# Splitting every 125-partition transfer as 120 + 5 partitions in place of 112 + 13

## The chip, the core and the metric

The kernel runs on one core of a Trainium2 chip. The metric is the time of one execution on the device, in microseconds (us). Each time is the median of several runs.

## What is computed

The reference is a small network of eight residual blocks over 3125 nodes with 256 features each and 50,000 directed edges (sorted by target). Layer normalisation precedes each block:

```
x = x + attention_4_heads(norm(x))          # L0 gnn, over the edges and self loops
x = x + mixture_of_8_experts(norm(x))       # L0 ffn, hidden 256, two best experts
x = x + two_attention_layers(norm(x))       # L1 gnn, 4 heads, then 1 head of 256
x = x + recurrence(norm(x))                 # L1 ffn
x = x + three_convolutions(norm(x))         # L2 gnn, adjacency product, bias, relu
x = x + mixture_of_8_experts(norm(x))       # L2 ffn, hidden 1024
x = x + one_convolution(norm(x))            # L3 gnn
x = x + mixture_of_8_experts(norm(x))       # L3 ffn, hidden 512
```

## The kernel before

3125 nodes are 25 tiles of 125 rows. Almost every array in SBUF therefore has 125 partitions (`P = 125`, `T = 25`), one node of a tile in each. All plain transfers are begun by SyncE, on one queue, in the order of its program; row gathers and scatters by index are begun by GpSimd on another.

- The first two attention layers (`by_edges`) go over 25 blocks of edges. GpSimd gathers 17 lists of 128 feature rows for a block (line 842). Beside it a class `Adjacency` builds the dense adjacency tile of each block and stores it in two arrays in DRAM: `NEG` (a mask, line 637) and `ADJ16` (counts as float16, line 639), 3125 numbers of two bytes in each partition.
- The third attention layer (`dense_attention`) loads both back (lines 1352, 1387 and 1486).
- The convolutions load `ADJ16` tile by tile into a ring of nine buffers (line 2444). In the three-layer one GpSimd adds the self loops to each tile as it lands (line 2454), so its instructions show when a tile is there.
- The features are stored for the gathers (line 769), x is loaded at the start in five parts (line 1969).
- A mixture first stores its normalised rows to `rows_x` in five parts (line 3779), then loads the rest of its second weights if it is the one with hidden size 1024 (line 3298), and runs 56 slots of 128 rows through the experts. GpSimd scatters each slot's result to `rows_y`. When the last scatter has landed (wait at line 3613), SyncE begins ten loads, two for each of five parts of five tiles (line 3619; line 3091 in the first mixture, where the following layer's front is joined to it). VectorE adds each part into x with ten operations (line 3729), and in the last mixture SyncE stores a part of the output when it has been added (line 3624).

All of these transfers go through one helper, `two_starts`. It begins the transfer in two pieces over partitions, each with its own completion count of 16, and everyone who waits for it waits for 32.

Of the kernel before, what the change touches and what calls it, by code (L numbers as in the profile page):

```python
# [5 lines left out]
P, T = 125, 25  # L6
# [117 lines left out]

def two_starts(e, out, src, sig):

    for lo, hi in ((0, 112), (112, P)):
        e.dma_start(out[lo:hi], src[lo:hi]).then_inc(*sig.by(16))  # L128


# [363 lines left out]
class Adjacency:  # L494
# [139 lines left out]
    def sync(self, e, t):  # L634
        m = self.order(t)
        e.wait_ge(*self.neg_made.at(m + 1))
        two_starts(e, self.k.NEG[t], self.mask[:, :], self.neg_out)
        e.wait_ge(*self.cols_out.at(7 * (m + 1)))
        two_starts(e, self.k.ADJ16[t], self.cols[:, :, :].rearrange("p t i -> p (t i)"), self.adj_out)
# [117 lines left out]
class ToTable:  # L757
# [5 lines left out]
    def sync(self, e):  # L763
        h = self.heads
        rows = self.k.HR.rearrange("(t p) c -> p t c", p=P)
        for i0, i1 in ((0, 4), (4, 7), (7, 10), (10, 12), (12, 13)):
            t0, t1 = 2 * i0, min(2 * i1, T)
            e.wait_ge(*h.out.at(i1))
            two_starts(e, rows[:, t0:t1, :], h.HA[:, t0:t1, 0:h.terms + h.H], self.out)
# [3178 lines left out]
```

## Time and profile before

| | |
|---|---|
| Median of 3 runs | 4234.94 us (4234.51 to 4237.27) |
| Time of the profiled execution | 4236.11 us |
| Its span in the profile | 4234.3 us |
| TensorE matmuls busy | 3471.0 us, 82% of the span |
| VectorE busy | 2679.7 us, 63% |
| GpSimd busy | 1295.1 us, 31% |
| Plain queue (q1) | 116800 packets, 251.73 MB, 21.5% of what 16 DMA engines could do |

The profile's page gives busy time by engine, the chain that ended last, and the costliest groups of instructions. PE is TensorE, DVE VectorE, ACT ScalarE, POOL GpSimd, SPq the sequencer of SyncE. A time in a row is counted from the start of the span. "DMA share" is the mean busy share of the core's 16 DMA engines in a stretch; it is made from packet durations, so it can come out a little over 1.

### The profile page before, as it was taken

The page shows a single profiled execution, that of the slowest core. Times are in us where ns is not written, and L with a number is a line of the kernel's source. Part 1 is how long each engine was busy: PE and PEld are TensorE (multiplying, and loading weights), DVE is VectorE, ACT ScalarE, POOL GpSimd, SP SyncE. Part 2 cuts the span into 40 slices and gives each one's busy share as a digit, 9 for nine tenths or more (in the row PEclk, how much of TensorE's full clock was granted, in tenths as well). Part 3 has the DMA queues.
Part 4 walks back from the last instruction along what each step waited for, and adds up shares of the span by engine and source line. Part 5 has one row for each costly group of instructions (what it writes and reads, how often), then busy time and mean ns, then how long its engine had stood idle before and what let it go on. Part 6 is the DMA issues. An engine that isn't in the chain of part 4 may idle for free. (4 is left out here: it accounts for less than half of the span.)

```text
span 4234.3 us, 63960 instructions
## 1 busy us (share of the span) xinstructions
PE 3471.0 (82%) x22424; PEld 2902.0 (69%) x22424; DVE 2679.7 (63%) x6841; ACT 1627.8 (38%) x4215; POOL 1295.1 (31%) x1348
## 2 busy tenths in 40 slices
PE   4777775775777788998899999799997899959695
PEld 3556664653555566784888888655597799959695
DVE  6799997556888878973888888732136333353544
ACT  2354442232444435561666666621102233310231
POOL 6777771637777720000000000000000222200263
PEclk8778877986888889999999999899998999979898
DMA  5455553344555555600000000245555211163424
GB/s 158 136 146 161 146 151 102 97 136 127 144 159 145 151 151 152 147 1 15 1 1 1 2 1 1 47 108 125 141 141 182 76 37 38 32 153 97 150 72 131
DMA packets 178026, 419.53 MB, mean 99 GB/s; under 512 B 58688, under 2 KB 103410, under 8 KB 177216
## 3 DMA queue, kind: packets, MB, share of 16 engines
q1 hardware_dynamic: 116800, 251.73, 21.5%
q0 software_dynamic: 60928, 164.04, 13.7%
q8 instruction: 162, 2.65, 0.3%
q14 instruction: 136, 1.11, 0.1%
HBM read 331.25 MB, written 84.36 MB: 98 GB/s over the span
## 5 line engine op out<-in xcount | busy, mean ns | idle before, releaser
L842 POOL DMA_INDIRECT sb<-features,sb x850 | 840.1, 988 | 262.3 <-issue 258.1
L2137 PE MATMUL ps<-sb 128*128 128x125 f32 x5184 | 635.6, 279 | 71.2 <-DVE sb L2201 70.1
L2137 PEld LDWEIGHTS ps<-sb 128*128 128x128 f32 x5184 | 595.0, 192 | 111.8 <-DVE sb L2201 110.5
L3742 ACT ACTIVATE sb<-ps,sb 128x128 f32<-128x128 f32 x784 | 220.9, 376 | 545.0 <-PE ps L3662 545.0
L2168 ACT ACTIVATE sb<-ps 128x125 f32<-128x125 f32 x1296 | 330.6, 273 | 223.2 <-PE ps L2137 194.7
L1211 PE MATMUL ps<-sb 128*125 128x260 f32 x1700 | 388.0, 387 | 13.1 <-PEq L1209 12.7
L3662 PE MATMUL ps<-sb 128*128 128x128 f32 x3136 | 383.1, 277 | 3.1 <-DVE sb L3705 1.8
L1211 PEld LDWEIGHTS ps<-sb 128*125 128x125 f32 x1700 | 320.0, 190 | 94.0 <-issue 41.4
L3662 PEld LDWEIGHTS ps<-sb 128*128 128x128 f32 x3136 | 369.0, 194 | 3.9 <-DVE sb L3705 2.1
L3676 PE MATMUL ps<-sb 128*128 x1568 | 368.0, 381 | 2.6 <-ACT sb L3742 2.6
L3676 PEld LDWEIGHTS ps<-sb 128*128 128x128 f32 x1568 | 286.7, 191 | 35.4 <-issue 3.1
L3639 POOL DMA_INDIRECT rows_y<-sb x168 | 191.6, 1141 | 382.0 <-DVE sb L3717 368.3
L1527 PE MATMUL ps<-sb 125*125 125x257 f32 x1250 | 282.0, 388 | 20.2 <-DVE sb L1594 12.4
L619 PE MATMUL ps<-sb 128*125 128x392 bf16 x850 | 242.4, 466 | 66.5 <-PEq L617 65.1
L1527 PEld LDWEIGHTS ps<-sb 125*125 125x125 f32 x1250 | 238.5, 192 | 62.0 <-DVE sb L1594 15.5
L2545 PE MATMUL ps<-sb 125*128 125x500 f16 (+1 forms) x1400 | 275.7, 352 | 0.0
L2565 PE MATMUL ps<-sb 125*125 125x256 f16 x2500 | 273.4, 273 | 0.0
L2565 PEld LDWEIGHTS ps<-sb 125*125 125x125 f16 x2500 | 273.1, 136 | 0.3
L619 PEld LDWEIGHTS ps<-sb 128*125 128x125 bf16 x850 | 163.7, 201 | 133.7 <-issue 74.6
L3698 DVE COPY sb<-sb 128x512 f32 (+2 forms) x168 | 133.3, 793 | 179.3 <-PE ps L3662 178.7
L1017 DVE TENSOR_TENSOR sb<-sb,ps 128x1560 f32<-128x1560 f32 x150 | 244.3, 1684 | 1.7
L3717 DVE TENSOR_TENSOR sb<-ps,sb 128x256 f32<-128x256 f32 x168 | 71.4, 425 | 268.8 <-PE ps L3676 268.8
(380 smaller groups left out, 5296.3 us busy)
## 6 DMA issues: line engine op xcount, KB each, us to landing
sb<-adj SPq DMA_DIRECT2D x125, 683.6 KB
neg<-sb SPq DMA_DIRECT2D x25, 683.6 KB
adj<-sb SPq DMA_DIRECT2D x25, 683.6 KB
sb<-neg SPq DMA_DIRECT2D x25, 683.6 KB
sb<-in_L_ffn_W SPq DMA_DIRECT2D x16, 1024.0 KB
sb<-features,sb POOLq DMA_INDIRECT x850
sb<-rows_y SPq DMA_DIRECT2D x20, 560.0 KB
sb<-adj SPq DMA_DIRECT2D x125, 79.3 KB
```

Source lines behind the costliest of these rows:

```text
L619: r = e.matmul(k.PS[0:P, 2 + x, 0:392], dt[:, w, :], self.hots[w % 4][:, 392 * x:392 * x + 392], start=w == 0, stop=w == W - 1)
L842: e.indirect_dma_start(hgs[i % 4][:, w, :], None, k.HR, indirect(ids[i % 3][:, w:w + 1])).then_inc(*hg_in[i % 4].by(16))
L1017: e.tensor_tensor(v, v, shares[:, w0:w1, :].unsqueeze(3).broadcast_to([128, w1 - w0, 4, 65]), ALU.mult).then_inc(scaled_token.sem, 1)
L1211: m = e.matmul(k.PS[0:P, sum_bank(u), 0:260], wides[u % 2][:, w, :], hgs[u % 4][:, w, 0:260], start=w == 0, stop=w == W - 1)
L1527: m = e.matmul(k.PS[0:P, n, 0:257], work[u % 7][:, n * P:n * P + P], HA[:, j, 0:257], start=j == 0, stop=j == T - 1)
L2137: return e.matmul(sums(n, g)[:, 0, :], V[:, y, (4, 0, 5, 1, 2, 3)[g], :], self.old_h(n)[:, y, :], start=False, stop=y == 1, skip_group_che ...
L2168: e.activation(Gt[:, row, :], sums(n, g)[:, 0, :], ACT.Tanh if row >= 4 else ACT.Sigmoid).then_inc(acted, 1)
L2545: m = e.matmul(out, part[:, j, 128 * h:128 * h + 128], self.ads[:, first:first + len(ts), j * P:j * P + P], start=j == 0 and x == 0, stop= ...
L2565: m = e.matmul(self.k.PS[0:P, v % 2, 0:D], self.ads[:, self.slot(v), j * P:j * P + P], part[:, j, :], start=j == 0 and x == 0, stop=j == T ...
L3662: m = e.matmul(hidden(n, c), w1s[n % deep][:, x, c, :], xts[n % 2][:, x, :], start=x == 0, stop=x == 1)
L3676: m = e.matmul(k.PS[:, 5 + n % 2, 0:D], hts[n % 2][:, c, :], w2f[:, bass.ds(v * (nh * D) + c * D, D)], start=c == 0, stop=c == nh - 1)
L3742: m = e.activation(hts[n % 2][:, c, :], hidden(n, c), ACT.Gelu, bias=cons[n % 4][:, c:c + 1])
```

## The change

The helper cuts after 120 partitions in place of 112. The first piece grows from 112 to 120 partitions and the second shrinks from 13 to 5. The number of transfers, their bytes, their order, and every wait stay as they are.

```
 def two_starts(e, out, src, sig):
 
-    for lo, hi in ((0, 112), (112, P)):
+    for lo, hi in ((0, 120), (120, P)):
         e.dma_start(out[lo:hi], src[lo:hi]).then_inc(*sig.by(16))
```

## Rows read from the trace of the kernel before

**Rows 1.** The page, DMA queues: packets, MB, share of 16 engines.

```profile
q1 hardware_dynamic: 116800, 251.73, 21.5%
```

**Rows 2.** The DMA view of 3742.6 to 3772 us: packets, MB, share.

```profile
DMA packets 1507, 6.55 MB, mean 223 GB/s; under 512 B 248, under 2 KB 504, under 8 KB 1504
...
q1 hardware_dynamic: 1504, 6.51, 91.0%
```

**Rows 3.** The DMA view of 4192 to 4232 us.

```profile
q1 hardware_dynamic: 4810, 9.60, 86.6%
```

**Rows 4.** Windows: stretch, busy us of the engines (instructions), PEclk, DMA share, GB/s.

```profile
3243.00:3260.00 17.00, 9.19 (x82) 8.64 (x80) 13.97 (x47) 10.03 (x21) 0.00 (x0) 0.85 1.03 411
...
3714.00:3734.00 20.00, 0.00 (x0) 0.00 (x0) 13.60 (x34) 0.00 (x0) 0.00 (x0) 0.50 1.02 245
...
3955.00:3962.00 7.00, 0.00 (x0) 0.00 (x0) 6.73 (x11) 0.00 (x0) 0.00 (x0) 0.50 0.89 367
...
4196.00:4220.00 24.00, 0.00 (x0) 0.00 (x0) 16.09 (x40) 0.00 (x0) 0.00 (x0) 0.50 1.03 265
4220.00:4228.00 8.00, 0.00 (x0) 0.00 (x0) 4.14 (x11) 0.00 (x0) 0.00 (x0) 0.50 0.94 320
```

**Rows 5.** Windows of one us at the end of a burst of loads.

```profile
3733.00:3734.00 1.00, 0.00 (x0) 0.00 (x0) 1.00 (x4) 0.00 (x0) 0.00 (x0) 0.50 0.87 220
3734.00:3735.00 1.00, 0.00 (x0) 0.00 (x0) 1.00 (x4) 0.00 (x0) 0.00 (x0) 0.50 0.89 251
3735.00:3736.00 1.00, 0.00 (x0) 0.00 (x0) 1.00 (x4) 0.00 (x0) 0.00 (x0) 0.50 0.47 128
```

**Rows 6.** Waits of the whole span on DMA: total us, times, longest.

```profile
POOL sb L2454 <- DMA sb<-adj: 437.6, 75, 43.0
...
DVE sb L3729 <- DMA sb<-rows_y: 23.6, 9, 10.0
...
DVE sb L1433 <- DMA sb<-neg: 2.1, 2, 1.1
```

**Rows 7.** Windows of the edge layers and the convolutions.

```profile
1600.00:1700.00 100.00, 83.01 (x359) 69.39 (x360) 85.88 (x91) 57.61 (x69) 0.00 (x0) 0.90 0.63 157
...
3000.00:3200.00 200.00, 200.00 (x1486) 157.23 (x1484) 53.51 (x139) 19.93 (x46) 14.23 (x35) 1.00 0.51 134
...
83.00:600.00 517.00, 389.52 (x2188) 300.33 (x2188) 441.00 (x1032) 224.16 (x347) 393.98 (x403) 0.78 0.53 148
```

**Rows 8.** Timeline of POOL: start, us; when two of the first tiles are there.

```profile
2746.03 0.40 POOL L2454 TENSOR_TENSOR sb<-sb 125x125 f16<-125x125 f16 x1 [3.19 <-DMA sb<-adj]
...
2759.42 0.40 POOL L2454 TENSOR_TENSOR sb<-sb 125x125 f16<-125x125 f16 x1 [2.95 <-DMA sb<-adj]
```

**Rows 9.** The gathers of the edge layers (line 842): who waits.

```profile
L842 POOL DMA_INDIRECT sb<-features,sb x850 | 840.1, 988 | 262.3 <-issue 258.1
```

**Rows 10.** Timelines of SPq and DVE, the first mixture's parts.

```profile
898.75 8.56 SPq L128 DMA_DIRECT2D sb<-rows_y  x20
...
907.88 3.26 DVE L3103 SCALAR_TENSOR_TENSOR sb<-sb 125x256 f32<-125x256 f32 x8 [12.09 <-PEq L105]
...
913.03 2.46 DVE L3103 SCALAR_TENSOR_TENSOR sb<-sb 125x256 f32<-125x256 f32 x6
...
928.58 2.46 DVE L3103 SCALAR_TENSOR_TENSOR sb<-sb 125x256 f32<-125x256 f32 x6
```

**Rows 11.** Timeline of SPq and POOL, the mixture of hidden size 1024.

```profile
3266.89 20.48 SPq L3298 DMA_DIRECT2D sb<-in_L_ffn_W  x8
...
3288.53 1.40 POOL L3634 DMA_INDIRECT sb<-rows_x,sb  x1 [53.24 <-POOLq L105]
```

**Rows 12.** Timeline of DVE, the parts of that mixture's result.

```profile
3716.62 4.05 DVE L3729 SCALAR_TENSOR_TENSOR sb<-sb 125x256 f32<-125x256 f32 x10 [5.08 <-DMA sb<-rows_y]
...
3737.33 4.05 DVE L3729 SCALAR_TENSOR_TENSOR sb<-sb 125x256 f32<-125x256 f32 x10 [0.74 <-DMA sb<-rows_y]
```

**Rows 13.** The chain that ended last, its end.

```profile
4200.39 19.75 DMA sb<-rows_y
```

## The prediction

> **What bounds the kernel now.** I read the page first. The plain queue moves 251.73 MB in 116800 packets and fills 21.5% of the DMA engines' time [rows 1]. Transfers are thus no bound on average, and the question is where one ends a wait.
>
> The windows by stage answer most of it. In the edge layers GpSimd begins gathers without pause: of its 262.3 us idle before line 842, 258.1 are its own issue time [rows 9], at a DMA share of 0.53 [rows 7]. In the convolutions TensorE is busy all of 200 us at a share of 0.51, and in the dense attention layer the share is 0.63 [rows 7]. A transfer may get a third slower there and still be hidden.
>
> The waits of the whole span come next [rows 6]. GpSimd waits 437.6 us for adjacency tiles, but it only adds self loops there and TensorE, which uses the result, never stops. VectorE waits 23.6 us for `rows_y`, which is the end of the two later mixtures, and the chain that ended last has the same transfer in it for 19.75 us [rows 13]. These bursts are the exposed ones.
>
> **What the cut decides.** How many DMA engines share a transfer, and how many rows the busiest one has, can be counted. In the stretch of eight adjacency tiles and one weight load the queue has 1504 packets, 248 of them under 512 B [rows 2]. Eight tiles have 1000 rows and the weight load 256. The 248 small ones left are 8 x 29 + 16. At the end of the kernel ten loads of 125 rows and five stores of 625 pieces make 4375, and 4810 - 4375 = 435 = 15 x 29 [rows 3]. So each 125-row transfer ends in 29 small packets and a 128-row one in 16. I read this as 16 engines for the piece of 112 (7 rows each), 13 for the piece of 13 (one each): the busiest has 8 rows, three have 7. The end of a burst agrees: the share falls to 0.87 and 0.89 before it collapses to 0.47, about 13 of 16 [rows 5].
>
> After the change the same pattern, an equal number of rows on each of at most 16 engines, gives 15 engines with 8 rows and 5 engines with one more. The busiest have 9, five of the 16; ten have 8; one has none. If 120 rows were instead dealt unevenly over 16 engines, the busiest would still have 9.
>
> The Trainium skill, "DMA: Bandwidth & Descriptors", section "Why a DMA increments its semaphore by 16 and not by 1", has the rule: the largest number of engines up to 16 that divides the slowest dimension, and always the lowest-numbered ones. The counted 29 and 16 agree with it. By it alone, 9 rows in place of 8 make every exposed transfer 12.5% longer, which is the upper bound below.
>
> **What a row costs.** The loads of 5120-byte rows run at 245 GB/s [rows 4], 15.3 GB/s for each of 16 engines, or 334 ns a row. Weight loads of 128 rows run at 411 GB/s, which would be 199 ns for such a row. Stores of 125 rows run between 320 and 367 GB/s, 223 to 256 ns. So loads with the 112 + 13 cut are slowed by something that 128-row loads don't meet. Also, when three engines have run dry the total stays at 220 to 251 GB/s [rows 5]: part of the limit is shared, and fewer engines each run faster.
>
> **The sum**, each term with the work around it:
>
> - *Two bursts of ten loads* (after the mixtures of hidden size 1024 and 512). VectorE waits before each part, from 5.08 us for the first to 0.74 for the last [rows 12], so a later landing goes straight through. If the engine is the limit, the busiest has 10 rows more at 334 ns, +3.3 us. If the total is, the old burst is 70 rows at 334 ns plus 10 at 13 engines' share of 235 GB/s (283 ns), 26.2 us; the new one is 80 rows at 15 engines' share of 245 (313 ns), then 10 rows on five free engines at 199 ns, 27.1 us: +0.9. The rows speak for both; I take 2.0 each, +4.0.
> - *Five output stores at the very end.* The DMA engines work from the loads into the stores without a gap (shares 1.03 and 0.94) [rows 4], so one more row of 5120 bytes in each counts: 5 x 0.22 to 0.26 us, +1.2, bounds 0.5 and 1.3.
> - *Five stores of normalised rows before the mixture of hidden size 1024.* They stand in the queue before the last eight weight loads, whose issue takes 20.48 us and ends just before GpSimd may begin the experts at 3288.53 [rows 11]. Five more rows, +1.1, bounds 0 and 1.3. In the last mixture the same stores run at 367 GB/s between 3955 and 3962 beside 6.73 us of VectorE work on the placing of the rows, which the block's end waits for [rows 4]: nothing; without that cover 1.1.
> - *The first mixture's ten loads.* SyncE begins them from 898.75 on, and like the other bursts they take some 26 us; VectorE starts on the parts at 907.88, 913.03 and so on to 928.58 with no DMA wait [rows 10]. By the share of tiles before them (10 of 25, 22 of 25) these land at about 910 and 922, 3 and 6 us early. +12.5% is covered. Without that cover it is 3.3.
> - *Adjacency tiles at the front of the convolutions.* They land 13.39 us apart for four, 3.35 each [rows 8]; at 9/8 that is 3.77. With the convolutions' share at 0.51 a tile is needed only half as often: nothing.
> - *Mask and adjacency stores in the edge layers*, loads of x, masks in the dense layer: beside GpSimd's gathers or under VectorE's work; the two mask waits are 2.1 us together [rows 6]. With the ends of stages, +0.5, bounds 0 and 1.5.
>
> Together 4.0 + 1.2 + 1.1 + 0.5 = +6.8 us. The profiled execution took 4236.1 us, 1.8 more than its span, and would take 4242.9. The median of the runs shown is 1.2 lower, so 4234.9 + 6.8 = 4241.7; I say 4242 us. The terms' bounds give +2.3 to +10.7, so 4237 to 4246 for this case.
>
> **The rivals.**
>
> *A, engines meet (slower).* Loads reach only 245 of 411 GB/s, which looks like several engines writing to one entrance of SBUF at a time. With equal shares of eight rows that meeting could be regular, every row with one partner, 2 x 199 = 398 ns. A transfer then takes 8 x 398 plus a contended ninth of about 500, 3.7 us against 2.7. Twenty exposed loads cost 20 us, the first mixture's cover of 3 us is used up (+2), and stores and ends 2.8: +25, 4260. For it: the unexplained slowness is there already. Against it: in unequal queues (9 rows beside 8) partners drift apart. The Trainium skill, "SBUF — State Buffer", section "Door 1: The DMA port swizzle", gives each port two groups of four partitions, 32 apart. By that map contiguous eights make engines four apart share both their ports, which speaks for A; no trace here shows which rows an engine has.
>
> *B, the slowness goes away (faster).* 128-row loads give each engine eight rows, and 120 over 15 does too. If the eights, and not the sevens, are what runs at 199 ns, a load takes 9 x 199 ns = 1.8 us. In the burst after hidden size 1024 VectorE's waits shrink by 1.8 us for the first part and the later 4.5 of waiting vanish; at the end of the kernel similarly 1.8 + 4.0, and 1.5 from the earlier drain of the stores; the other terms stay: -13.6 + 1.6, about -12, so 4223. It decides from a row time of 8/9 x 334 = 297 ns downward. Against it: five engines still meet at the last five partitions, and the eights of a 128-row tile may be dealt differently.
>
> *C, nothing to see.* The shared limit rules throughout, extra rows fall in gaps: 0 to +2, 4236. Rows 5 speak for it, the gapless end of the kernel against it.
>
> **How the numbers follow.** About 0.2% (8.5 us) is what a measurement can tell from no change. Forecast 0.48, of which 0.16 beyond +8.5; A 0.22; B 0.18, of which 0.02 within 8.5; C 0.12. Faster 0.16, within 0.2% 0.02 + 0.12 + 0.32 = 0.46, slower 0.16 + 0.22 = 0.38. The range takes in most of B and the nearer half of A, 4224 to 4256.
>
> **What the changed profile would show.** The plain queue has 265 such transfers; 20 small packets in place of 29 in each leave 116800 - 2385 = 114415 packets. Ends of bursts fall to a share near 0.3 (five engines), with middles near 0.94. Adjacency tiles land 3.5 to 3.8 us apart; over 4.2 it is A, under 3.0 it is B. VectorE's last wait in each burst grows by about 2 us. The prediction is wrong if row time changes with the cut, if the queue of one late engine holds up SyncE's issue somewhere before a weight load, or if a landing in the edge layers turns out to hold a block.

## The result and the profile after

The changed kernel takes 4244.98 us (median of 9 runs, 4240.08 to 4247.2), the kernel before on the same chip 4234.51 us: a ratio of 1.0024 with an interval of 1.0014 to 1.0034, some 10 us slower. Its profiled execution took 4245.34 us with a span of 4243.7, 9.4 more than before.

The page's DMA queues show how the rows are dealt (compare [rows 1]):

```profile
q1 hardware_dynamic: 114415, 251.72, 22.5%
```

That is 2385 packets fewer, nine in each of the 265 transfers, as forecast. The waits of the whole span on DMA (compare [rows 6]):

```profile
DVE sb L3729 <- DMA sb<-rows_y: 30.5, 10, 11.2
...
DVE sb L1433 <- DMA sb<-neg: 4.8, 4, 2.7
...
DVE sb L154 <- DMA sb<-in_x: 2.7, 1, 2.7
...
DVE sb L3103 <- DMA sb<-rows_y: 0.8, 1, 0.8
```

The wait for `rows_y` is longer by 6.9 us. The two last lines have no partner before: the loads of x and of the first mixture were less well covered than I had thought. The burst after hidden size 1024, in the timelines of SPq and DVE (before, SPq began at 3708.95 us; compare [rows 12]):

```profile
3709.48 7.50 SPq L128 DMA_DIRECT2D sb<-rows_y  x20
```
```profile
3717.89 4.05 DVE L3729 SCALAR_TENSOR_TENSOR sb<-sb 125x256 f32<-125x256 f32 x10 [5.84 <-DMA sb<-rows_y]
...
3740.48 4.05 DVE L3729 SCALAR_TENSOR_TENSOR sb<-sb 125x256 f32<-125x256 f32 x10 [1.08 <-DMA sb<-rows_y]
```

The kernel enters the burst 0.5 us late and starts the last part 3.15 late (3737.33 before): 2.6 us lost in it. I had forecast that the last wait grows by about 2 us; it grew by 0.34 only, and the delay is spread over the five waits (5.84, 1.83, 1.53, 1.96 and 1.08 us in place of 5.08, 1.18, 1.53, 1.07 and 0.74). The windows after the burst show another microsecond. First the kernel before, then the one after, both counted from the first matmuls of the next block (columns as in [rows 4]):

```profile
3753.00:3756.00 3.00, 3.00 (x15) 2.54 (x13) 0.89 (x3) 0.71 (x2) 0.00 (x0) 0.96 0.99 233
```
```profile
3756.00:3759.00 3.00, 3.00 (x10) 2.38 (x10) 0.29 (x3) 0.53 (x2) 0.00 (x0) 0.66 0.97 219
```

TensorE, idle for 42 us ahead of this block in place of 40, is granted 0.96 of full speed in one and 0.66 in the other, both windows beginning 7.7 us after the block's first matmul. The same 16 matmuls of line 2498 take 4.99 us in place of 4.14. The longer idle time does not explain it. In two of the runs below, first the one with only the bursts changed and then the one with all but the bursts changed, the longer idle time goes with the shorter matmuls:

```profile
3748.76 2.08 PE L2464 MATMUL ps<-sb 128*128 128x256 f32 x4 [43.05 <-ACT sb L2623]
...
3755.67 4.26 PE L2498 MATMUL ps<-sb 128*125 128x256 f32 x16
```
```profile
3742.16 2.08 PE L2464 MATMUL ps<-sb 128*128 128x256 f32 x4 [38.32 <-ACT sb L2623]
...
3749.07 5.21 PE L2498 MATMUL ps<-sb 128*125 128x256 f32 x16
```

Over all 14 traces of this case the idle time is 38.3 to 43.1 us and these matmuls take 4.14 to 5.53 us, without a visible relation. So 0.9 us of this pair of traces is the clock's variation from one execution to the next, as far as can be told, and not a price of the change.

The last burst: SPq begins at 4196.84 (before 4192.59, so 4.25 late), and the last part starts at 4228.57. Before, the last two parts ran as one group of twenty operations from 4216.05 to 4224.21, so the last ten began at 4220.16:

```profile
4216.05 8.16 DVE L3729 SCALAR_TENSOR_TENSOR sb<-sb 125x256 f32<-125x256 f32 x20 [1.00 <-DMA sb<-rows_y]
```

The burst lost 4.2 us. From the end of the last sum to the end of the span it is 10.1 us before and 11.1 after. The whole account: 0.5 ahead of the first burst, 2.6 in it, 1.1 in the block behind it, 4.2 in the last burst, 1.0 in the output's stores make 9.4. It is the account of one pair of traces: where the code up to the first burst is the same as before, four traces enter it between 3708.95 and 3710.99 us, so the 0.5 us can't be told from nothing.

```profile
4228.57 4.05 DVE L3729 SCALAR_TENSOR_TENSOR sb<-sb 125x256 f32<-125x256 f32 x10 [0.39 <-DMA sb<-rows_y]
```

Windows of the middle and of the end of the first of these bursts after the change (compare [rows 4, 5]):

```profile
3715.00:3735.00 20.00, 0.00 (x0) 0.00 (x0) 12.14 (x30) 0.00 (x0) 0.00 (x0) 0.50 0.96 235
...
3738.00:3739.00 1.00, 0.00 (x0) 0.00 (x0) 1.00 (x4) 0.00 (x0) 0.00 (x0) 0.50 0.27 97
```

The middle stands near 15 of 16 engines, the end near five of 16 (0.27, at 97 GB/s), as forecast. The middle's rate fell as well. In windows of 18 us that hold no stores it is 236 from 246 GB/s in the one burst and 230 from 255 in the other.

### The profile page after: what moved, and what is told of

Read it like the earlier page. It is cut to its first block and busy times, and to the rows that moved or that the text cites. A ratio compares the mean times of both kernels' runs of the same rounds, so it can differ in the third digit from the quotient of the medians.

```text
span 4243.7 us, 63960 instructions
## 1 busy us (share of the span) xinstructions
PE 3482.4 (82%) x22424; PEld 2910.5 (69%) x22424; DVE 2683.2 (63%) x6841; ACT 1626.8 (38%) x4215; POOL 1293.9 (30%) x1348
## 5 line engine op out<-in xcount | busy, mean ns | idle before, releaser
L1211 PE MATMUL ps<-sb 128*125 128x260 f32 x1700 | 388.4, 388 | 10.2 <-PEq L1209 9.7
```

What stands on the lines that cost most here:

```text
L1211: m = e.matmul(k.PS[0:P, sum_bank(u), 0:260], wides[u % 2][:, w, :], hgs[u % 4][:, w, 0:260], start=w == 0, stop=w == W - 1)
```

## The experiments

All have the helper with another cut, unless a line is named. "Before" below is the kernel before on the same chip. A burst's length is counted from SPq's first start to the start of VectorE's last ten operations. "Tiles" are the second to the eighth adjacency tile at the front of the convolutions, 3.45 us apart before. The runs were made on several chips, where the median of the kernel before was 4234.5 to 4239.2 us; ratios compare one chip with itself, and from the traces mainly lengths are compared.

**One line alone, and all but that line.** The helper gets the cut as a parameter:

```
-def two_starts(e, out, src, sig):
-    for lo, hi in ((0, 112), (112, P)):
+def two_starts(e, out, src, sig, cut=112):
+    for lo, hi in ((0, cut), (cut, P)):
...
-    two_starts(e, got[:, n, c, :, :], best[...], got_in[n])        # line 3619
+    two_starts(e, got[:, n, c, :, :], best[...], got_in[n], 120)
```

This is the second run. The first has 120 everywhere and 112 in line 3619.

> The changed kernel, but the ten loads after each of the two later mixtures are cut 112 + 13 again; all other transfers stay 120 + 5. Theory (the cost is the later landing of these two bursts, 3.6 and 4.2 us by the two traces): about 7.8 of the 10.5 us go, so +2 to +3 us against the kernel before, ratio 1.0006; in its profile the last of the final mixture's waits ends within 1 us of the kernel before. Rival (many small later landings in the edge layers, the first mixture and the convolutions add up): most of the loss stays, +6 us or more, ratio 1.0014 or more.

> The kernel before, but only the ten loads after each of the two later mixtures are cut 120 + 5; 20 of 265 transfers. Theory (these two bursts carry the loss): +7 to +8 us, ratio 1.0018. Rival (small landings everywhere): +2 to +4 us, ratio below 1.001. If the two experiments' losses do not add to the whole loss of 10 us, the transfers change each other's timing and neither theory is complete.

Measured: 1.0005 (0.9996 to 1.0014) with the bursts left as they were, 1.0016 (1.0007 to 1.0026) with only the bursts changed. Both fit the theory and not the rival, and the two losses add to 0.21%, which agrees with the whole 0.24% within the intervals. By the centres, twenty of 265 transfers carry about two thirds of the loss.

**The same number of rows on the busiest engine, cut otherwise; one row more, cut otherwise.** `(0, 80), (80, P)` gives 15 engines 8 rows (5 + 3); `(0, 105), (105, P)` gives ten engines 9 (7 + 2).

> Every transfer cut 80 + 45: 16 engines with 5 rows, then 15 engines with 3 rows, so again 8 rows on the busiest engine as with 112 + 13, now on fifteen engines. 31 small packets in each transfer, 117330 packets on the plain queue. Theory (the number of rows on the busiest engine decides): like the kernel before, within 3 us. Rival (the time of a row depends on how many neighbouring partitions an engine has, because engines meet at one entrance of SBUF): the pace of the adjacency tiles moves from 3.4 us by more than 0.3 us either way, and the time by 5 us or more.

> Every transfer cut 105 + 20: 15 engines with 7 rows, then 10 engines with 2 rows, so 9 rows on the busiest engine as with 120 + 5, but on ten engines, 7 on five, none on one. Theory A (the busiest engine's rows at an unchanged row time): like the change, +10 us, tile pace 3.8 us. Theory B (the total rate is shared, so that late engines run faster when few are left): the ten late engines get less speed than the five of the change at the end of a burst, so +11 to +15 us. Rival (the eights of the 120 piece are slow by themselves, the sevens are not): clearly less than the change, +3 to +6 us.

Measured: 80 + 45 took 1.0021 (1.0011 to 1.003) with tiles 3.82 us apart, 105 + 20 only 1.0005 (0.9996 to 1.0014) with tiles 3.43 apart. The theory that only the rows of the busiest engine count falls: eight rows cost as much here as nine do in the change, and nine rows cost next to nothing.

**Where the blocks lie.** `(0, 5), (5, P)`, and `(0, 13), (13, P)` as its control.

> All transfers as (0, 5) and then (5, 125). The counts of rows on each engine are those of the change (five engines with 9, ten with 8), but the fifteen blocks of eight rows begin at partition 5, 13, 21 and so on in place of 0, 8, 16. Theory M (where the blocks of rows lie sets how the engines meet, and so what a row costs): with the blocks off the multiples of eight the row gets cheaper, the adjacency tiles at the front of the convolutions land under 3.6 us apart in place of 3.84, the two bursts lose less than 2.5 us each in place of 3.6 and 4.2, ratio 1.0003 to 1.0015. Rival S (the size of the blocks alone sets it, wherever they begin): tiles 3.8 apart, bursts +3.6 and +4.2, ratio 1.0020 to 1.0028, as the change.

> All transfers as (0, 13) and then (13, 125): the counts of rows are those of the kernel before (13 engines with 8, three with 7), with the sevens beginning at 13 in place of 0. It is the control of the run with the five rows first. Theory M: a small change of the row's time is possible, but sevens drift over the positions anyway, so tiles land 3.3 to 3.6 us apart (3.45 before) and the ratio is 0.9994 to 1.0006. Rival O (what counts is whether the small piece stands first in each engine's queue): a shift of the bursts by over 1 us each, of the same sign as in the run with the five rows first.

Measured: 1.0033 (1.0021 to 1.0045) with five first, tiles 4.04 us apart; 1.0004 (0.9995 to 1.0013) with thirteen first, tiles 3.33 apart. Moving the eights off the multiples of eight helped nothing; theory M falls. The bursts last as with the change (31.8 and 32.1 us). What is lost beyond it comes earlier: the kernel enters the first of them 4.1 us late, with mask waits of 7.9 us in the dense attention layer (2.1 before).

**Stores alone** (lines 637, 639, 769, 3624 and 3779 with 120).

> The kernel before with the five lines that store (masks, adjacency, features, normalised rows, output) cut at 120 and all loads at 112. Theory: the loss of the change is in its loads, and of the stores only the five at the very end count, about 1.0 us: ratio 1.0000 to 1.0005, the bursts' waits as before. Rival: the stores in the edge layers and before the mixture of hidden size 1024 cost as well (my prediction gave the latter 1.1 us): ratio 1.0006 or more, with the first gatherless stage after the edge layers shifted by over 1 us.

Measured: 1.0005 (0.9996 to 1.0014). Its bursts last 27.5 us both, as before (28.4 and 27.6), and the end behind the last sum 11.1 us in place of 10.1. That microsecond is all that its trace ties to the stores; the interval doesn't exclude a little more.

**More rows, fewer engines.** `(0, 117), (117, P)`.

> All transfers as 117 and 8 rows: 13 engines with 9 rows, of which eight get a tenth, and three engines with none. Theory M with the count: blocks of nine rows are off the multiples of eight and cost as the sevens or less (260 to 320 ns of 5120 bytes), ten rows of them make 2.6 to 3.2 us for a load in a burst, adjacency tiles 3.4 to 3.9 us apart, ratio 1.0000 to 1.0020. Rival E (thirteen engines carry less, each at the rate seen with 112 + 13): a load takes 10 x 334 = 3.3 us, bursts +6 us each, tiles over 4.2 apart, ratio 1.0030 or more. The five last stores have two rows more than before either way, about +2 us.

Measured: 1.0008 (0.9999 to 1.0017). Ten rows on the busiest engines, and the bursts last 28.2 and 28.3 us. Windows of 18 us in them show why:

```profile
3716.00:3734.00 18.00, 0.00 (x0) 0.00 (x0) 12.14 (x30) 0.00 (x0) 0.00 (x0) 0.50 0.83 251
4200.00:4218.00 18.00, 0.00 (x0) 0.00 (x0) 12.14 (x30) 0.00 (x0) 0.00 (x0) 0.50 0.83 254
```

Thirteen engines carry as much as sixteen did, 19.4 GB/s each in place of some 15.8. Rival E's bursts of +6 us don't come, so for these loads it is not each engine by itself that sets the rate; a limit shared by all would fit. For the adjacency tiles (rows of 6250 bytes) it is otherwise: they land 3.79 us apart, nearly as slow as with the change (3.84). That lies in theory M's range, as does the ratio, though the theory itself falls with the run before.

**The order of 80 and 45, and eleven rows.** `(0, 45), (45, P)` and `(0, 104), (104, P)`.

> All transfers as (0, 45) and then (45, 125): the same two sizes as in the run with 80 + 45, in the other order, so again 8 rows on fifteen engines. That run lost 0.21%, its tiles in the convolutions landed 3.82 us apart and its bursts took 22 us. Theory P (two engines that are at rows behind one entrance of SBUF share its rate, and where the blocks lie decides how often they meet; worked out with the row of 199 ns for an engine alone at its entrance, the mean load of 5120-byte rows comes to 2.68 us for 80 + 45, 2.44 for 45 + 80, 2.44 for 112 + 13 and 2.98 for 120 + 5): with the 45 rows first the loss is gone, tiles land 3.3 to 3.55 us apart, the last burst is as before, ratio 0.9992 to 1.0006. Rival Z (the size of the blocks alone, fives being slow): tiles 3.75 or more apart, ratio 1.0015 to 1.0027, as with 80 + 45.

> All transfers as 104 and 21 rows: 13 engines with blocks of 8 rows, seven of which get 3 more, so the busiest seven have 11 rows and three engines none. Theory P gives a mean load of 5120-byte rows of 3.2 us (2.44 for the cut of before): tiles about 4.2 us apart or more, each burst 5 us or more longer, ratio 1.0025 or more. Rival T (the total rate of all engines limits and the rows of the busiest hardly count, since 117 + 8 with ten rows on eight engines cost only 0.08%): tiles under 3.8 us apart, bursts under +2.5, ratio under 1.0015.

Measured: 45 first 1.002 (1.0011 to 1.0029), tiles 3.42 us apart, bursts 29.3 and 29.7 us. Theory P had the tiles right and the ratio wrong; the two orders cost the same. 104 + 21 took 1.0096 (1.008 to 1.0111). Rival T falls. Theory P had named no upper end, but its 1.0025 is far from this, and of the bursts (30.4 and 36.6 us) only the second is 5 us longer or more. The trace is that of the slowest of the four runs (4294.54 us, median 4280.89). In it the tiles land 4.6 us apart, and the mask loads of the dense attention layer have lost their cover (2.1 us before):

```profile
DVE sb L1433 <- DMA sb<-neg: 32.0, 7, 10.0
```

**The two halves of the cost**, both in line 3619 alone: three pieces `(0, 112, 120, 125)` with the wait in line 3724 raised to 96 (blocks of seven, a ninth row on five engines), and 120 rows without the rest (blocks of eight and no ninth row).

> The kernel before with only the twenty loads of the two bursts (line 3619) begun as three pieces, 112, 8 and 5 rows, and the wait for a part raised from 64 to 96. Sixteen engines keep their blocks of seven; the first five have 9 rows, three have 8, eight have 7. Theory N (the ninth row on five engines is the cost, 10 rows of 0.31 us a burst): each burst +3 us as in the run with 120 + 5 at this line, last wait chain 24 to 26 us, ratio 1.0012 to 1.0022. Rival K (the blocks of eight in step are the cost, and a ninth row among blocks of seven is not): bursts within 1 us of before, the last burst's transfer part of the chain 19 to 21 us, ratio 0.9996 to 1.0006.

> The kernel before with only the loads of line 3619 cut to their first 120 rows, in one piece; the five last rows of every tile are left out of these loads and of VectorE's sum (x keeps its value there). Fifteen engines have 8 rows each and nobody a ninth. Theory N: 10 rows less than with 120 + 5 on the busiest engines and 5 rows in 125 less in all, so each burst ends as before or up to 1 us earlier, ratio 0.9992 to 1.0003. Rival K: blocks of eight still cost, each burst 1.5 to 3 us later than before though four per cent less is loaded, ratio 1.0006 to 1.0014.

Measured: 1.0007 (0.9998 to 1.0016) with three pieces, between the theories, with bursts at most 2.0 and 2.2 us above the 27.8 that 112 + 13 takes in the mean. Part of that may be the third start, which lengthens SyncE's issue of a burst from 8.3 to 10.5 us. 120 rows only: 1.001 (1.0001 to 1.0019), in rival K's range, with bursts 2.9 and 1.0 us above the mean where K had 1.5 to 3; theory N, which had them no later than before, does not fit. Windows show where each is late. Three pieces:

```profile
3716.00:3734.00 18.00, 0.00 (x0) 0.00 (x0) 11.30 (x29) 0.00 (x0) 0.00 (x0) 0.50 1.03 245
4199.50:4217.50 18.00, 0.00 (x0) 0.00 (x0) 11.08 (x28) 0.00 (x0) 0.00 (x0) 0.50 1.03 249
```

120 rows only:

```profile
3716.00:3734.00 18.00, 0.00 (x0) 0.00 (x0) 11.71 (x30) 0.00 (x0) 0.00 (x0) 0.50 0.96 214
4203.20:4221.20 18.00, 0.00 (x0) 0.00 (x0) 12.14 (x30) 0.00 (x0) 0.00 (x0) 0.50 0.98 236
```

With the sevens the middle nearly keeps its rate and the burst is late through its end; with the eights alone the middle is slow, more so in one burst (214 GB/s) than in the other (236).

**All bursts and ends side by side.** The two columns of lengths are those after hidden size 1024 and 512; the rate is that of 18 us in the middle of each; the end is from the last sum to the end of the span.

| loads of line 3619 | busiest engine, rows | bursts, us | GB/s | stores of the output | end, us |
|---|---|---|---|---|---|
| 112 + 13 (before) | 8 | 28.4, at most 27.6 | 246, 255 | 8 rows | 10.1 |
| 112 + 13 (stores alone changed) | 8 | 27.5, 27.5 | 260, 254 | 9 | 11.1 |
| 112 + 13 (all but the bursts changed) | 8 | 27.2, 28.6 | 259, 243 | 9 | 11.1 |
| 13 + 112 | 8 | at most 27.5, at most 28.2 | 254, 252 | 8 | 10.0 |
| 120 + 5 (the change) | 9 | 31.0, 31.7 | 236, 230 | 9 | 11.1 |
| 120 + 5 (only the bursts) | 9 | 32.0, 32.5 | 226, 223 | 8 | 10.0 |
| 5 + 120 | 9 | 31.8, 32.1 | 230, 227 | 9 | 11.1 |
| 120 only | 8 | 30.7, 28.8 | 214, 236 | 8 | 10.3 |
| 112 + 8 + 5 | 9 | at most 29.8, at most 30.0 | 245, 249 | 8 | 9.9 |
| 105 + 20 | 9 | at most 27.6, 29.1 | 254, 244 | 9 | 11.2 |
| 117 + 8 | 10 | 28.2, 28.3 | 251, 254 | 10 | 12.2 |
| 80 + 45 | 8 | 30.4, 30.0 | 229, 234 | 8 | 9.9 |
| 45 + 80 | 8 | 29.3, 29.7 | 234, 234 | 8 | 10.2 |
| 104 + 21 | 11 | 30.4, 36.6 | 247, 202 | 11 | 13.3 |

("At most": VectorE ran on without a wait there.) The tiles land 3.24 to 3.45 us apart in the six traces whose loads are cut 112 + 13 or 13 + 112, 3.42 with 45 + 80, 3.43 with 105 + 20, 3.79 with 117 + 8, 3.79 and 3.84 with 120 + 5, 3.82 with 80 + 45, 4.04 with 5 + 120 and 4.62 with 104 + 21. No cut beats 112 + 13 by more than can be measured: all ratios are above 1, and those of 13 + 112, 105 + 20 and 117 + 8 have 1 in their intervals.

## Why the prediction was right, and where its sizes were off

The sign was right, and so were the packets and the places of the loss, the two bursts and the last stores. 4244.98 lies in the range of 4224 to 4256. The forecast of 4242 was 3 us short, and the ratio's centre lies just beyond the 0.2% that I had set as measurable.

- *How rows are dealt*: right. The packet count came out to the unit, and for the other cuts too: 80 + 45 has two small packets more in a transfer, 116800 + 265 x 2 = 117330 as on its page; 117 + 8 has eight fewer, 114680. The Trainium skill's rule ("DMA: Bandwidth & Descriptors", section "Why a DMA increments its semaphore by 16 and not by 1") gives each of these counts, and the traces agree.
- *Two bursts, +2.0 each*: the step that was mis-sized. "The rows speak for both; I take 2.0 each" averaged between an engine's limit (+3.3) and a shared one (+0.9). The four bursts with 120 + 5 last 31.8 us in the mean, the eight with 112 + 13 or 13 + 112 27.8: +4.0. The shared bound failed because it kept 245 GB/s in the middle; the four middles with 120 + 5 have 229 in the mean, the eight others 253. The engine's bound was nearly right. At these rates a row takes 5120 x 15 / 229 = 335 ns after, close to my 334, and 5120 x 16 / 253 = 324 ns before; 90 rows at the one less 80 at the other are +4.2 us.
- *But the price of a row is not the engine's own*, and that was the sign of being wrong that I had set. With 117 + 8 a row takes 5120 x 13 / 252 = 264 ns: at 334 ns its 20 more rows would cost 6.7 us a burst, and they cost 0.4. Nor is it the one engine less. That alone would give 253 x 15 / 16 = 237 GB/s, but 105 + 20 has 15 engines in its large piece too and keeps 249. The two halves run alone give +2.0 us (120 only) and at most +2.1 (three pieces). As two bursts with one cut differ by up to 1.9 us, this says that the eights cost something by themselves; how much each half carries is not shown.
- *After the burst*: the 0.9 us that TensorE's 16 matmuls took longer is in my pair of traces, but not tied to the change (see the result).
- *Output stores, +1.2*: measured 1.0. And the table shows the rule behind it over all cuts: 9.9 to 10.3 us of end with 8 rows on the busiest engine, 11.1 to 11.2 with 9, 12.2 with 10, 13.3 with 11. Five stores at 1.1 us for a row is 0.22 us each, the lower price that I had taken.
- *Stores before the mixture of hidden size 1024, +1.1*: wrong. The stores' issue takes 11.43 us where it took 12.51, and GpSimd begins the experts at 3288.30, earlier than [rows 11]. From the first store's issue to the experts GpSimd takes 32.8 to 34.6 us in the five traces with 9 rows in these stores, and 33.7 to 36.5 in the five with 112 + 13 or 13 + 112, so no run shows this term. The stores' issue after (before, 12.51 us from 3254.33):

```profile
3253.70 11.43 SPq L128 DMA_DIRECT2D rows_x<-sb  x10
```

- *First mixture hidden, with 3 us to spare*: nearly wrong. A part that I put at 910 was waited for at 913.85 (compare [rows 10]). I had counted by share of the tiles from SPq's start; in the later bursts the second part starts 12.9 us behind it, which from 898.75 gives 911.6 and half the cover.

```profile
913.85 2.46 DVE L3103 SCALAR_TENSOR_TENSOR sb<-sb 125x256 f32<-125x256 f32 x6 [0.82 <-DMA sb<-rows_y]
```

- *Adjacency tiles hidden, 3.77 us apart*: right. The second to the eighth land between 2746.33 and 2769.35, 3.84 apart, and the first burst behind the convolutions begins 0.5 us late only. How far the cover of such transfers reaches shows in the dense attention layer: its mask waits are 4.8 us with the change, 7.9 with 5 + 120 (4.04 us a tile) and 32.0 with 104 + 21 (4.6).

```profile
2746.33 0.40 POOL L2454 TENSOR_TENSOR sb<-sb 125x125 f16<-125x125 f16 x1 [3.16 <-DMA sb<-adj]
...
2769.35 0.40 POOL L2454 TENSOR_TENSOR sb<-sb 125x125 f16<-125x125 f16 x1 [3.50 <-DMA sb<-adj]
```

- *Edge layers, x, masks, +0.5*: the kernel is 0.5 us late where the first burst begins, no more than traces of the same code differ there. VectorE waits 2.7 us for x's last part, but 3.5 less for the next thing (`in_dst`, 4.7 to 1.2), which gives it back.

*Luck.* The bursts cost about 8 us by the means (6.8 in the pair of traces) where I had 4.0, and the 1.1 for the stores before hidden size 1024 is nowhere to be seen. These misses have opposite signs. So it is in part luck that the forecast is only 3 us short.

*The rivals.* A (engines meet regularly, +25 us, tiles over 4.2 apart): not at its size. The blocks of eight with 120 + 5, 5 + 120 and 120 only do carry some 10% less (229, 228 and 225 GB/s against 253), but whether engines meeting is the reason no run shows. B (a row time of 297 ns or less): no, it is 335. C (a shared limit, nothing to see): it fits 117 + 8 and 105 + 20, and not 120 + 5.

*What stays open.* Why the total is some 250 GB/s with pieces of 112, 117 or 105 and some 230 with 120, 80 + 45 or 45 + 80 is not settled; 104 + 21 has 247 in one burst and 202 in the other. Theory P, built on engines that share an entrance, was right for the tiles with 45 first and wrong for the bursts with 45 first. The port map of the Trainium skill ("SBUF — State Buffer", section "Door 1: The DMA port swizzle"), on which P rests, is neither shown nor refuted by that: no trace here tells which rows an engine is at when. Two bursts with one cut differ by up to 2 us (120 only: 30.7 and 28.8), so differences under 1 us between cuts are left unread.

## What to carry to other kernels

For a split over partitions, write down how many engines each piece gets and the rows of the busiest one: the five stores at this kernel's end follow that count within 0.2 us. For the bursts of loads it is a poor guide (8 rows with 80 + 45 cost more than 10 with 117 + 8); the cut moves their rate by some 10%, and that has to be measured. Weigh a slower transfer first where something waits for it at the end of a stage: here 20 transfers of 265 carried about two thirds of the loss, and the covered ones cost nothing that can be told at some 10% slower (the change), some 4 us at 17% (5 + 120) and tens of us at a third (104 + 21).

## What the runs showed of the hardware that I had not expected

- Thirteen DMA engines moved as much as sixteen in a burst of loads: 251 and 254 GB/s with 117 + 8, against 246 and 255 with 112 + 13. The adjacency tiles did land later with it, 3.79 us apart in place of 3.45.
- The same 5120-byte loads run at 214 to 236 GB/s when the large piece has 120 rows on 15 engines, whether it begins at partition 0 or 5, and at 243 to 260 with 112 rows on 16.
- Five engines left alone at the end of a burst carry 97 GB/s, at least 19 each, a quarter more than in the middle (235 / 15 = 15.7).
- After an idle time of some 40 us TensorE's granted clock rises from 0.50 to 1.00 (1.2 to 2.4 GHz) sooner in some executions than in others. In a window of 3 us that begins 7.7 us after the block's first matmul it is 0.96 before and 0.66 after, and the same 16 matmuls took 4.14 us behind 39.7 and behind 43.0 us of idle time, 5.21 behind 38.3.
